# The gather of the next rows spread over four steps, and residual stores moved ahead in SyncE's turn

## The reference

```python
h = base_weight[x] + einsum('bsr,dr->bsd', lora_A.T[x], lora_B)     # embedding with a rank-16 addition
h = h + attention(layernorm(h))    # 16 heads of 32; low-rank q and kv (128 wide) with layer norms; causal
h = h + ffn(layernorm(h))          # shared expert + 8 of 16 routed experts, sigmoid gate

# attention
cq  = _layernorm(x @ W_dq, q_ln_g, q_ln_b);   Q = cq @ W_uq
ckv = _layernorm(x @ W_dkv, kv_ln_g, kv_ln_b); K, V = split(ckv @ W_ukv)
attn = softmax(where(causal, q @ k.T / sqrt(32), -inf))
return (attn @ v) @ W_o.T
```

## Time and profile before

| | |
|---|---|
| time, median of 3 runs | 2663.51 us (2663.29 to 2664.27) |
| profiled execution | 2662.18 us |
| its span | 2660.4 us |
| busy PE, PEld | 95%, 71% of the span |
| busy ACT, DVE, POOL | 69%, 64%, 42% |
| DMA queues: hardware (SyncE), software (GpSimd) | 20.4%, 2.5% of 16 engines |
| attention phase | the first 1,085 us or so |

### The profile page before, as it was taken

One profiled execution on the slowest core, in us unless ns is written; L12 is line 12 of the kernel. 1 busy time (PEld: TensorE's weight loads), 2 busy tenths in 40 slices (PEclk: granted clock), 3 DMA queues, 4 the chain that ended last, 5 costly groups with the idle time before them and its releaser, 6 DMA issues.

```text
span 2660.4 us, 49271 instructions
## 1 busy us (share of the span) xinstructions
PE 2530.0 (95%) x13120; PEld 1890.3 (71%) x13120; DVE 1695.1 (64%) x3742; ACT 1837.2 (69%) x4597; POOL 1129.0 (42%) x1275
## 2 busy tenths in 40 slices
PE   3899999999999999689999999999999999999999
PEld 2666666666666665467888888888888888888887
DVE  5666666666666665366765765676576567657655
ACT  1666677777777777376866876786686678668666
POOL 4333343334334432123644544454454445446445
PEclk8999999999999999789999999999999999999999
DMA  3222222222121211241222122132222213212221
GB/s 112 56 65 64 64 64 64 64 64 64 64 64 64 64 48 37 92 143 63 98 88 84 51 96 86 40 108 86 69 69 95 86 41 107 83 57 86 91 72 60
DMA packets 99750, 197.23 MB, mean 74 GB/s; under 512 B 10928, under 2 KB 10928, under 8 KB 99568
## 3 DMA queue, kind: packets, MB, share of 16 engines
q1 hardware_dynamic: 94576, 179.29, 20.4%
q0 software_dynamic: 5120, 17.31, 2.5%
HBM read 145.66 MB, written 50.86 MB: 74 GB/s over the span
## 4 chain that ended last, share of the span: by engine, by line
issue 29%; POOL 24%; PE 2%; DVE 1%; ACT 1%; POOLq 1%; DMA 0%; SPq 0%; DVEq 0%; ACTq 0%
POOL t_lo L1181 23%; POOL sh_lo L1181 1%; POOLq L1179 1%; DVE ps_u L1550 0%; DVE f_lo L1575 0%; DMA x<-h 0%; ACT x L1344 0%; DVE t L1557 0%; ACT t_hi L1399 0%; PE ps_g L1196 0%; PE ps_g L1198 0%; PE ps_u L1198 0%; PE ps_u L1196 0%; PE ps_u L1197 0%; PE ps_g L1197 0%
## 5 line engine op out<-in xcount | busy, mean ns | idle before, releaser
L1181 POOL TENSOR_TENSOR t_lo<-t,t_hi 128x512 fp32r<-128x512 f32 x512 | 665.1, 1299 | 423.5 <-ACT t_hi L1399 423.4
L395 POOL TENSOR_TENSOR probs<-probs,inv 128x512 f32<-128x512 f32 x256 | 265.1, 1041 | 577.1 <-DVE inv L803 577.1
L622 ACT ACTIVATE probs<-ps_s,nmax 128x128 f32<-128x128 f32 x1024 | 362.4, 371 | 153.1 <-DVE nmax L798 149.9
L1550 DVE TENSOR_TENSOR ps_u<-ps_u,square 128x512 f32<-128x512 f32 x512 | 357.0, 697 | 159.0 <-ACT square L1386 154.3
L1399 ACT ACTIVATE t_hi<-t 128x512 fp32r<-128x512 f32 x512 | 320.5, 626 | 119.9 <-PE ps_y L1198 69.0
L1557 DVE TENSOR_TENSOR t<-ps_u,w_all 128x512 f32<-128x512 f32 x512 | 354.0, 691 | 60.7 <-DMA w_all<-w_rows 20.7
L1382 ACT ACTIVATE square<-ps_g 128x512 f32<-128x512 f32 x544 | 319.8, 588 | 91.6 <-PE ps_g L1198 89.5
L1386 ACT ACTIVATE square<-square 128x512 f32<-128x512 f32 x544 | 344.2, 633 | 17.3
L513 PE MATMUL ps_s<-k_diag,qT 128*128 128x512 f32 x512 | 261.4, 592 | 0.0
L798 DVE TENSOR_REDUCE nmax<-ps_s 128x4 f32<-128x512 f32 x256 | 174.3, 681 | 126.5 <-PE ps_s L513 124.1
L1196 PE MATMUL ps_y<-t_hi,f_hi 128*128 128x512 f32 x512 | 209.9, 410 | 13.2 <-POOL t_lo L1181 13.0
(11 more groups left out here) (196 smaller groups left out, 5502.9 us busy)
## 6 DMA issues: line engine op xcount, KB each, us to landing
w_all<-w_rows SPq DMA_DIRECT2D x256, 256.0 KB, 3.1
h<-h SPq DMA_DIRECT2D x64, 256.0 KB, 2.7
res<-h SPq DMA_DIRECT2D x64, 256.0 KB, 2.8
h<-res SPq DMA_DIRECT2D x64, 256.0 KB, 2.0
x<-h SPq DMA_DIRECT2D x16, 1024.0 KB, 5.7
fres<-h SPq DMA_DIRECT2D x16, 1024.0 KB, 7.3
out<-fres SPq DMA_DIRECT2D x64, 256.0 KB, 2.7
fres<-in_w_ffn SPq DMA_DIRECT2D x14, 512.0 KB, 3.6
```

Source lines behind the costliest of these rows:

```text
L395: pool.tensor_tensor(probs[:, s % 4, :, :], probs[:, s % 4, :, :], inv[:, s % 4, :].rearrange("p (h o) -> p h o", o=1).to_broadcast([P, HP ...
L622: e = act.activation(probs[:, s % 4, j, :], ps_s[:, s % 2, j, :], ACT.Exp, bias=nmax[:, s % 4, j:j + 1], accum_out=total[:, s % 4, j:j + 1])
L1181: pool.tensor_tensor(lo, t[:, t_slot(j), :], hi.bitcast(F32), ALU.subtract).then_inc(t_lo_done, 1)
L1550: dve.tensor_tensor(dst, product, square[:, j % 2, :], ALU.mult).then_inc(t1_done, 1)
```

## The change

On GpSimd, `gather` is cut in two: `pick` copies the indices, and `gather(g, t)` issues the transfer of one tile. `GATHER_AT` goes from step 10 to step 7: indices and tile 0 in step 7, tiles 1, 2 and 3 in steps 8, 9 and 10. In turn -2 the clearing of `k_diag` stands behind the first of them. On SyncE, the four residual stores of a turn go ahead of everything else in it.

```diff
-GATHER_AT, RSTD_AT, C_RSTD_AT = 10, 6, 1
+GATHER_AT, RSTD_AT, C_RSTD_AT = 7, 6, 1
...
             def turn(n):
+                if has_part(n, "h", 0):
+                    for t in range(TILES):
+                        bank, before = place(n, "h", t)
+                        wait_alone(sp, work_free[bank], DRAINS * (before + 1), sp_passed)
+                        sp.dma_start(h2[bass.ds((n + 2) * TOK + t * P, P), :],
+                                     h[:, t, :]).then_inc(res_kept[t], 16)
                 for i in range(TILES + 1):
...
                                      h2[bass.ds(n * TOK + t * P, P), :]).then_inc(res_loaded[t], 16)
-                    if has_part(n, "h", 0):
-                        bank, before = place(n, "h", t)
-                        wait_alone(sp, work_free[bank], DRAINS * (before + 1), sp_passed)
-                        sp.dma_start(h2[bass.ds((n + 2) * TOK + t * P, P), :],
-                                     h[:, t, :]).then_inc(res_kept[t], 16)
...
-                    if step == GATHER_AT and has_part(n, "h", 0) and not is_turn(n, GROUPS - 3):
-                        wait_gathered(n + 2)
-                        drained(pool, n, "h", TILES - 1)
-                        gather(n + 3)
-                        if is_turn(n, -2):
+                    if GATHER_AT <= step < GATHER_AT + TILES and has_part(n, "h", 0) and not is_turn(n, GROUPS - 3):
+                        if step == GATHER_AT:
+                            wait_gathered(n + 2)
+                            drained(pool, n, "h", TILES - 1)
+                            pick(n + 3)
+                        gather(n + 3, step - GATHER_AT)
+                        if is_turn(n, -2) and step == GATHER_AT:
                             pool.wait_ge(w_lo_done, len(W_PIECES))
                             pool.memset(k_diag[:, :, :, :, :], 0.0).then_inc(k_zeroed, 1)
```

More of the change, by code:

```diff
@@ L340, in turn @@
                     t = i - 1
-                    if t < 0:
-                        continue
-                    if slots_of(n):
+                    if t >= 0 and slots_of(n):
                         wait_alone(sp, stored[t], 16 * n, sp_passed)
@@ L374, in _, with pick, gather @@
             pool.wait_ge(tok_step, 4)
-            def gather(g):
+            def pick(g):
                 pool.tensor_copy(tok_now[:, :], tok_fix[:, bass.ds(g * TILES, TILES)]).then_inc(tok_picked, 1)
                 wait_alone(pool, tok_picked, g + 1, pool_passed)
[L379 to L383, removed]
+            def gather(g, t):
+                pool.indirect_dma_start(
+                    out=gath[:, t, :], out_offset=None, in_=table,
+                    in_offset=bass.IndirectOffsetOnAxis(ap=tok_now[:, t:t + 1], axis=0),
+                ).then_inc(gathered[t], 16)
             def wait_gathered(g):
@@ L413, in turn @@
                         newton_of(2 * NEWTON_OPS * (n + 1) + NEWTON_OPS, 2 * TILES)
-            gather(0)
+            pick(0)
+            for t in range(TILES):
+                gather(0, t)
             for n in (-2, -1, 0):
```

## The result

| | before | after |
|---|---|---|
| median | 2663.4 us (4 runs, 2659.47 to 2664.27) | 2637.8 us (4 runs, 2637.29 to 2638.47) |
| profiled execution | 2662.18 us | 2637.29 us |

The ratio is 0.9907, with an interval of 0.989 to 0.9924: faster by 25.6 us. That is 4.8 us above the 2633 forecast, inside its range. In other comparisons (a comparison is a set of runs of several kernels taken together on one chip) the kernel before took 2631 us, and there the change makes it 6.6 us slower.

A forecast was written before the change was run, and what follows sets the result against it. The PE queue, busy 95% of the span, was taken as the bound, so gains come only from its waits. 2662.18 - 31.2 (stall) + 1.1 (prologue) = 2632.1, median 2633; own range 2629 to 2641, whole range to 2653.

The forecast's parts named there:

- The stall: Step 12 of turns 1 to 12: falls to turn 0's 5.33 us once PE reports are not late, -31.2 us.
- Only where gathers and SyncE's transfers are in flight together: Around step 11: the claimed condition for late PE reports, drawn from turns 0, 6 and 13; no size of its own.
- The control "turn 0": Turn 0 has the gathers but no SyncE transfer then, and step 12 takes 5.33 us; offered as evidence for the cause.
- D: Rival: late reports have another cause that stays, a place in the program; only the prologue is left, 2664.6 us; chance 0.11.
- Remaining one gather beside one load: Step 10's last gather beside the load of residual tile 3: taken to cost 0.
- B: Rival: one gather beside one SyncE transfer is enough to hold PE reports; half the stall kept, 2649 us; chance 0.20.
- C: Rival: single gathers meeting SyncE transfers add up, 3.5 us a turn; slower, 2675 us; chance 0.07.
- Residual stores first: SyncE's queue: four stores a turn leave steps 7 to 11, nothing behind them comes late; cost 0.
- Spreading on GpSimd: Steps 7 to 10: slot 7 normalised 2.1 us later under 5 us of cover, slots 8 and 9 1.3 at most; cost 0.
- The prologue: Turn -2: three gathers behind the earlier clearing land late for VectorE's read; +1.1 us, bounds 0 to 2.2.
- the DMA story: Around step 11: PE reports late because of DMA traffic, against the skill's rule that DMA never contends; carries the 31.2 us.
- The sum: Whole kernel: profiled 2662.18 - 31.2 + 1.1 = 2632.1 us; median 1.33 above, 2633.4, so 2633.

The follow-up runs named there:

- f1: The kernel before run again unchanged, in another comparison, without the stall: 2631.44 us, ratio 1.0002 to the runs beside it.
- i1: Kernel before with residual stores first and residual loads moved to the next turn's head, four gathers still in step 10: 2640.0 us against 2666.02, 0.9902.
- h1: Kernel before with gathers spread over steps 7 to 10, clearing behind the fourth, SyncE's order unchanged; with the stall: 2631.11 us against 2665.29, 0.9875.
- i2: Kernel before with residual stores first and the four gathers in a row in step 7 instead of 10; with the stall: 2636.88 us, 0.9891.
- e3: Kernel before with only SyncE's order changed (residual stores first), four gathers still in step 10; without the stall: 2632.05 us, ratio 1.0.
- e4: Kernel after, with the clearing of k_diag behind the first gather also waiting for all four xn operations: 2632.96 us (one run).

## Why the prediction was right, and where it was not

**The stall, -31.2.** Measured -32.7 in turns 1 to 12. Sizing it by turn 0's 5.33 us was right (5.29). That reports of the PE were late, and not its work, is borne out by each trace with the stall. That this term came out also rests on luck: the first comparison was one of the three with the stall. The cause was told too simply. "Only where gathers and SyncE's transfers are in flight together" is wrong both ways: f1 has both and no stall, i1 has a stall and no transfers. The control "turn 0" thus did not show what I took it to show. It differed from the loop turns in a second thing, which I had passed over: its first gather starts 0.36 us behind the maximum of slot 10, in turns 1 to 12 it starts 0.33 ahead of it. Which of its differences keeps turn 0 free is not shown. Shown is: there must be a condition outside the program (three comparisons of five had it); given that, a row of four gathers in step 10 starts the stall, SyncE's transfers lengthen it, and neither single gathers beside loads and stores (h1) nor a row in step 7 (i2) start it. h1, i1 and i2 are two runs and one trace each, but in each trace all 12 turns agree. That the condition could be absent, and the change then worth less than nothing, I had not thought of. No rival had it: D named another cause, but one that stays in the kernel after.

**Remaining one gather beside one load, 0.** Right: h1 and the kernel after both have turns of 62.57. Rivals B and C fall.

**Residual stores first, 0 by themselves.** Right (e3, 1.0). In the stall they are worth 6.0 us by the medians, 6.5 by the maxima.

**Spreading on GpSimd, 0 with 5 us of cover.** Right in its price. Slot 7 is normalised 6.0 us behind its maximum (483.72 to 489.76) instead of 4.0; the maxima of slots 8 to 10 keep their distances of 4.83, 5.49 and 5.77 us to the hundredth. But the term looked only at who waits for GpSimd. It missed that the delayed slot 7 now runs beside xn and holds VectorE for 1.58 us a turn; by this, slot 8 is normalised 1.6 us later (4.26 behind its maximum in place of 2.69), not the 1.3 at most that I had reckoned. That this fell into waits and cost nothing was luck: the prediction has no reason for it.

**The prologue, +1.1.** This is the step that failed: it measured +6.35, outside its bounds of 0 to 2.2, and is why the time came out 4.8 high. I asked only what the early clearing makes late on GpSimd's own queue. That part was worked out well enough: in e4, where it stands alone, the rows were read at 47.45 against 47.6. But I did not look at what runs on VectorE in the microseconds into which the 6.96 us of clearing moved. The row stood in the trace of the kernel before (timeline of VectorE):

```profile
31.29 1.91 DVE L730 TENSOR_SCALAR xn<-h,moments,nw 128x512 f32<-128x512 f32 x4 [3.61 <-POOL nw L83]
```

It ends at 33.20, with the clearing now to start at about 33.3 in place of 37.10: close enough to have asked what happens if they meet. The rows alone would not have given the answer: in the kernel after, an undisturbed xn would have ended at 33.42 (31.51 + 1.91), 0.09 ahead of the recorded start of the clearing, and still was held; in e4 the recorded start is 0.05 later, and xn was free. The fourth xn was held for 7.3 us more than its 0.54, and xn is what the PE waits for. Then the gathers, late by their 1.1, were hidden behind it.

The Trainium skill (SBUF — State Buffer, "Who interferes with whom") names what fits this: VectorE and GpSimd share a pair of ports, and a form of VectorE's `tensor_scalar` can need it for the whole instruction. I had read that rule only against the DMA story and not against my own edit list. The trace agrees with it here, on both sides: the tensor_scalar xn went from 1.91 to 9.22 us beside the clearing, and the xT_lo subtraction, whose other input lies in PSUM, kept its 0.69 (e4). In turns 1 to 12 the same tensor_scalar was held beside a normalisation of GpSimd. Its other half, that DMA never contends with a compute engine, stands beside reports of the PE that come 0.8 to 4.0 us late near gathers. What holds these reports is not settled by any run: the PE's own instructions did not lengthen.

**The sum.** -31.2 + 1.1 = -30.1 was forecast between the profiled executions, -24.9 measured: 5.2 from the prologue, 1.5 from scatter behind turn 13, -1.5 from the stall.

**Left open.** What the condition is under which the kernel before has the stall, and why step 10 is open to it and step 7 hardly. No run has two or three gathers in a row, so how long the row must be is not known. Between comparisons the program was the same, and the chip once too.

## What to carry to other kernels

When a long GpSimd instruction (a clearing, a copy) moves, or is delayed, list what VectorE runs in the stretch it moves into, not only what is queued behind it; here one such meeting cost 6.35 us and twelve others were hidden. Indirect gathers issued one per step beside other work took no more time here than four in a row, and were free of a stall that four in a row had in one step of the turn and not in another. And a stall that is seen in one set of runs may be missing in the next with the same program: before crediting a change with it, run the kernel before again in another place.

## What was not expected of the hardware

- The kernel before has two times, 2631 and 2665 us, 1.3% apart. Each held through a whole comparison (up to 31 runs), and both were seen on one chip.
- With the stall, VectorE and ScalarE start on the PE's finished tiles 0.8 to 4.0 us late, where 0.03 is usual, while four indirect transfers are issued on GpSimd in step 10, and the late starts fall at places 0.7 us apart in the row; SyncE's transfers beside it triple the loss (10.8 to 32.7 us over 12 turns).
- A clearing of 6.95 us on GpSimd held one VectorE operation of 0.54 us for 7.85 (kernel after), and let three others of 0.69 through beside it (e4). A normalisation of 1.06 us did the same in a small way in each of turns 1 to 12 (1.96 in place of 0.54); gathers did not (i2).
